# Cross-attention of a Perceiver layer on one core: row-tiled scores, own keys as a third chunk, row sums by ones

## The reference

```python
# x (64, 32, 128), context (64, 257, 256): 64 sequences, 32 queries, 257 context keys, 16 heads of 8
qkv = (x @ w_qkv.T).reshape(B, N, 3, H, D).transpose(2, 0, 3, 1, 4)
q, k, v = (qkv[0], qkv[1], qkv[2])
kv = context.reshape(B, N_c, 2, H, D).transpose(2, 0, 3, 1, 4)
k = jnp.concatenate([kv[0], k], axis=2)          # 257 context keys and the sequence's own 32
v = jnp.concatenate([kv[1], v], axis=2)
attn = jax.nn.softmax(jnp.einsum('bhnd,bhmd->bhnm', q * scale, k), axis=-1)
out = jnp.einsum('bhnm,bhmd->bhnd', attn, v)
out = out.transpose(0, 2, 1, 3).reshape(B, N, C) @ w_proj.T + b_proj
```

## Time and profile before

| what | value |
|---|---|
| median of 3 runs | 752.95 us (750.12 to 755.46) |
| the profiled execution | 755.94 us, of which the span is 754.2 us |
| mean granted TensorE clock in the span | 0.912 |
| TensorE busy | 622.8 us, 83% |
| VectorE, ScalarE, GpSimd busy | 465.4, 316.8, 399.6 us |
| sequence 0's first score, sequence 63's first score | 33.74, 341.36 us |

### The profile page before, as it was taken

The page is one execution under the profiler, slowest core; times in us unless marked ns, Lnnn a source line. Parts: engine busy times, 40 slices in busy tenths (PEclk is TensorE's granted clock), DMA queues, the critical chain, the costliest instruction groups (busy, mean ns, idle before and its releaser), DMA issues. The chain is left out here.

```text
span 754.2 us, 14892 instructions
## 1 busy us (share of the span) xinstructions
PE 622.8 (83%) x4426; PEld 428.6 (57%) x4426; DVE 465.4 (62%) x919; ACT 316.8 (42%) x1003; POOL 399.6 (53%) x685
## 2 busy tenths in 40 slices
PE   3899999999999999997487888889528464777993
PEld 2577777777777777775122222223216254766993
DVE  6077777777777777776628487696654912343446
ACT  3555555655555665552223151504015322343550
POOL 3155555555555555551535849373526666666540
PEclk9999999999999999999559998999956767998997
DMA  5014452121111112110000000000001011111216
GB/s 161 3 44 134 133 133 60 52 56 56 56 56 53 48 54 56 56 42 2 1 0 0 0 1 0 0 1 0 1 0 56 0 29 45 44 40 43 39 37 171
DMA packets 30472, 33.26 MB, mean 44 GB/s; under 512 B 3498, under 2 KB 20996, under 8 KB 30436
## 3 DMA queue, kind: packets, MB, share of 16 engines
q1 hardware_dynamic: 27940, 27.68, 13.0%
q0 software_dynamic: 2496, 5.12, 2.5%
HBM read 28.13 MB, written 4.65 MB: 43 GB/s over the span
## 5 line engine op out<-in xcount | busy, mean ns | idle before, releaser
L594 PE MATMUL psum<-kT,q_heads 128*128 128x289 f32 x512 | 145.9, 408 | 0.8 <-ACT kT L482 0.8
L639 DVE COPY pT<-psum 128x512 f32<-128x512 f32 x128 | 86.5, 676 | 73.3 <-PE psum L554 73.3
L499 ACT ACTIVATE probs<-psum,neg_max 128x289 f32<-128x289 f32 x256 | 126.1, 497 | 12.7 <-DVE inv_sum L672 2.3
L659 DVE TENSOR_REDUCE neg_max<-psum 128x2 f32<-128x578 f32 x128 | 96.7, 755 | 21.8 <-PE psum L594 19.8
L427 POOL TENSOR_TENSOR probs_own<-probs,ones 128x128 f32<-128x128 f32 x64 | 25.8, 404 | 134.9 <-ACT probs L499 134.9
L594 PEld LDWEIGHTS psum<-kT,q_heads 128*128 128x128 f32 x512 | 87.3, 190 | 16.1 <-issue 1.0
L554 PE MATMUL psum<-ident,probs 128*128 128x128 f32 x512 | 79.0, 277 | 0.9 <-ACT probs L499 0.8
L554 PEld LDWEIGHTS psum<-ident,probs 128*128 128x128 f32 x512 | 64.3, 152 | 11.3 <-ACT probs L499 1.6
L395 POOL TENSOR_TENSOR q_heads<-qT,head_scaled 128x512 f32<-128x512 f32 x64 | 67.2, 1050 | 6.1 <-ACT k_own L469 6.1
L479 ACT COPY pT_own<-psum 128x128 f32<-128x128 f32 x64 | 17.0, 266 | 119.6 <-PE psum L545 119.6
L836 POOL TENSOR_TENSOR read<-recep,state 128x496 f32<-128x496 f32 x32 | 44.7, 1397 | 39.6 <-DVE state L1058 39.6
(11 more groups left out here) (257 smaller groups left out, 1320.0 us busy)
## 6 DMA issues: line engine op xcount, KB each, us to landing
kv_in<-in_ctx SPq DMA_DIRECT2D x64, 256.0 KB
w_gate<-in_L_ffn_Wg SPq DMA_DIRECT2D x1, 1408.0 KB, 7.5
w_up<-in_L_ffn_Wu SPq DMA_DIRECT2D x1, 1408.0 KB, 6.7
x_res<-in_x SPq DMA_DIRECT2D x4, 256.0 KB, 3.7
v_left_in<-in_ctx SPq DMA_DIRECT2D x64, 2.0 KB
w_down<-in_L_ffn_Wd SPq DMA_DIRECT2D x2, 512.0 KB, 5.2
x_rows<-x_cen SPq DMA_DIRECT2D x4, 256.0 KB, 2.3
w_gate<-y_rows SPq DMA_DIRECT2D x4, 256.0 KB, 3.7
```

The costliest lines, as they stand in the source:

```text
L499: last = nc.scalar.activation(probs[:, par, gr, :], bank[S_BANK[h][k]][:, 0:KEYS], ACT.Exp, bias=neg_max[:, par, gr:gr + 1], accum_out=row ...
L594: last = pe.matmul(bank[S_BANK[h][k]][:, 0:KEYS], q_heads[:, par, HG * gr:HG * gr + HG, :].rearrange("p h n -> p (h n)"), kT[:, par, :], s ...
L639: nc.vector.tensor_copy(pT[:, par, h, :], bank[PT_BANK[h]][:]).then_inc(s_pT_out, 1)
L659: nc.vector.tensor_reduce(neg_max[:, par, 2 * h:2 * h + 2], psum[:, 2 * h:2 * h + 2, 0:KEYS], AX.X, ALU.max, negate=True).then_inc(s_max, 1)
```

## The change

- The scores: `q_heads` shrinks to 128 channels x (4 heads x 32 queries). A group of heads has its 32 channels on 32 partitions, and each of the four matmuls takes only those rows of `q_heads` and `kT` (32 rows, 128 columns), all four in one run and with one signal.
- The own 32 values of a sequence and the last context row's value lie on 33 partitions, from partition 0 for even and from 64 for odd sequences (`v_own`, copied in pairs to `v_now`). Their probabilities are turned by four transposes (`turn_own`) in the middle of `values`, and enter as a third chunk of 33 rows.
- The row sums are matmuls with `ones` as weights over the same three chunks, into columns 128 to 255 of `O_BANK`; the exponentials lose their accumulated output, and `inverse`, `spread` and the matmul of L574 go.
- The context's keys and values are two tiles and two DMAs (`k_in`, `v_in`). Keys are turned two sequences ahead, values are computed two behind; `first` and last steps that lack a part are written out (`PEELED`, `LAST`, `exists`).
- The copy of the first half of the probabilities goes from VectorE to ScalarE, as does the copy of `O_BANK` (`o_rows`); masking, sums over heads and the product with the inverse go to GpSimd, three and four sequences behind.
- The last context row's values are broadcast to 32 partitions per parity by two DMAs before the loop, and TensorE waits for them before it turns `k_left`. The own values' projection is 16 matmuls of 128 columns per block, in two halves and two banks; ScalarE and VectorE copy one half each.
- In the mixture of experts the ring of gathered token tiles, `NXS`, goes from 15 to 12. Some unused semaphores of the second block go.

The diff, cut to its core:

```diff
@@ tiles and the loop
-            kv_in = sb("kv_in", [P, NSLOT, KC, 2 * C], scope)
-            q_heads = sb("q_heads", [P, 2, H, N], scope)
+            k_in = sb("k_in", [P, NSLOT, KC, C], scope)
+            v_in = sb("v_in", [P, NSLOT, KC, C], scope)
+            q_heads = sb("q_heads", [P, 2, HG, N], scope)
...
+            def own_rows(par):
+                return slice(64 * par, 64 * par + N + 1)
@@ SyncE
+                left_rows = ctx_dram[:, NCTX - 1, C:2 * C].rearrange("(i r) c -> r i c", r=2)
+                for r in range(2):
+                    sp.dma_start(v_own_pairs[64 * r + N:64 * r + 2 * N, :, :],
+                                 left_rows[r:r + 1, :, :].broadcast_to([N, B // 2, C])).then_inc(s_left_in, 16)
...
+                def load_keys(b, u):
+                    if not first(b, NSLOT):
+                        sp.wait_ge(s_keys, b - NSLOT + 1)
+                    sp.dma_start(k_in[:, u, :, :], rows_of(b, slice(0, C))).then_inc(s_k_in[u], 16)
+                def load_values(b, u):
+                    if not first(b, NSLOT):
+                        sp.wait_ge(s_pv, b - NSLOT + 1)
+                    sp.dma_start(v_in[:, u, :, :], rows_of(b, slice(C, 2 * C))).then_inc(s_v_in[u], 16)
@@ GpSimd
+                def normalise(b, par):
+                    pool.wait_ge(s_o_rows, b + 1)
+                    g.tensor_tensor(o_masked[:], o_rows[:, par].rearrange("p s (h n) -> p s h n", h=HG),
+                                    head_in_group[:].unsqueeze(1).unsqueeze(3).broadcast_to([P, 2, HG, N]),
+                                    ALU.mult).then_inc(s_o_steps, 1)
...
+                def step(b, u):
+                    par = u % 2
+                    if exists(b + 1):
+                        ready_q(b + 1, 1 - par)
+                    if exists(b) and par == 0:
+                        ready_v(b, u)
+                    if exists(b - 4):
+                        attended(b - 4, par)
+                    if exists(b - 3):
+                        normalise(b - 3, 1 - par)
@@ ScalarE
                 def step(b, u):
                     par = u % 2
+                    if exists(b - 3):
+                        rows_out(b - 3, 1 - par)
+                    if exists(b - 1):
+                        probs_out(b - 1, 1 - par)
+                    if exists(b + 2):
+                        act.wait_ge(s_scores, b + 1)
+                        keys_out(b + 2, par)
+                    if exists(b):
+                        for h in range(2):
+                            act.wait_ge(s_max, 2 * b + (h + 1))
...
@@ TensorE
+                def keys(b, u):
+                    pe.wait_ge(s_k_in[u], loaded(b, u))
+                    if not first(b, 4):
+                        pe.wait_ge(s_own_out, b - 3)
...
+                def turn_own(b, par):
+                    start = KEYS - (N + 1) - 64 * par
+                    for gr in range(G):
+                        last = pe.transpose(KEY_BANK[0:KEYS - start, P * gr:P * gr + P], probs[:, par, gr, start:KEYS], ident[:])
+                    last.then_inc(s_own_T, 1)
+                def values(b, u, par, between=None):
+                    if not first(b, 1):
+                        pe.wait_ge(s_o_rows, b)
+                    if par == 0:
+                        pe.wait_ge(s_ready_v, b + 2)
+                    pe.wait_ge(s_v_in[u], loaded(b, u))
+                    pe.wait_ge(s_pT0_out, b + 1)
+                    pe.wait_ge(s_pT1_out, b + 1)
+                    pe.wait_ge(s_own_out, b + 1)
+                    mine = own_rows(par)
+                    for s in range(2):
+                        for c in range(KC):
+                            if s == 0 and c == 1 and between:
+                                between()
+                            for gr in range(G):
+                                rows = slice(N * gr, N * gr + N)
+                                pe.matmul(O_BANK[rows, P * s:P * s + P],
+                                          ones[:] if s else v_in[:, u, c, rows],
+                                          pT[:, par, gr // 2, P * (2 * (gr % 2) + c):P * (2 * (gr % 2) + c) + P],
+                                          start=(c == 0), stop=False, skip_group_check=True)
+                        for gr in range(G):
+                            rows = slice(N * gr, N * gr + N)
+                            last = pe.matmul(O_BANK[rows, P * s:P * s + P],
+                                             ones[mine, :] if s else v_now[mine, u // 2, rows],
+                                             pT_own[mine, P * gr:P * gr + P],
+                                             start=False, stop=True, skip_group_check=True)
+                    last.then_inc(s_pv, 1)
...
                 def step(b, u):
...
+                        pe.wait_ge(s_exp, 2 * b)
+                        for gr in range(G):
+                            rows = slice(N * gr, N * gr + N)
+                            last = pe.matmul(bank[S_BANK[gr]][:, 0:KEYS],
+                                             q_heads[rows, par].rearrange("p h n -> p (h n)"),
+                                             kT[rows, par, :], start=True, stop=True)
+                        last.then_inc(s_scores, 1)
+                    if exists(b + 2):
+                        keys(b + 2, (u + 2) % NSLOT)
+                    if exists(b - 1):
...
+                        turn_probs(b - 1, 1 - par, 1).then_inc(s_pT1, 1)
+                    if exists(b - 1) and exists(b - 2):
+                        pe.wait_ge(s_keys_out, b + 3 if exists(b + 2) else B)
+                        values(b - 2, (u + 2) % NSLOT, par, lambda: turn_own(b - 1, 1 - par))
...
+                        turn_probs(b, par, 0).then_inc(s_pT0, 1)
@@ VectorE: the two maxima of b, then for b - 1 the copy of the second half and of the own rows, then for b - 3 the inverse
+                        nc.vector.tensor_copy(pT[:, 1 - par, 1, :], bank[PT_BANK[1]]).then_inc(s_pT1_out, 1)
+                        nc.vector.tensor_copy(pT_own[mine, :], KEY_BANK[mine, :]).then_inc(s_own_out, 1)
+                        nc.vector.reciprocal(o_inv[:, 1 - par, :], o_sum[:, 1 - par, 1, :]).then_inc(s_o_inv, 1)
@@ mixture of experts
-            NXS = 15
+            NXS = 12
```

More of the change, by code:

```diff
@@ L439, in step @@
-                    if not first(b, 1):
-                        spread(b - 1, (u + 1) % 2)
-                for u in range(NSLOT):
-                    step(u, u)
+                    par = u % 2
[7 more added lines that the diff above has]
+                        normalise(b - 3, 1 - par)
@@ L452, in _ @@
-                pack_own(B - 1, 1)
-                spread(B - 1, 1)
+                for b in range(B - NSLOT, B + LAST):
+                    step(b, b % NSLOT)
             @block.scalar
@@ new lines, in rows_out, with probs_out @@
+                def rows_out(b, par):
+                    act.wait_ge(s_pv, b + 1)
+                    if not first(b, 2):
+                        act.wait_ge(s_o_steps, 2 * b - 3)
+                    nc.scalar.copy(o_rows[:, par], O_BANK[:, 0:2 * P].rearrange("p (s q) -> p s q", s=2)).then_inc(s_o_rows, 1)
+                def probs_out(b, par):
+                    act.wait_ge(s_pT0, b + 1)
+                    if not first(b, 2):
+                        act.wait_ge(s_pv, b - 1)
+                    nc.scalar.copy(pT[:, par, 0, :], bank[PT_BANK[0]]).then_inc(s_pT0_out, 1)
@@ L526, in _ @@
                     pe.matmul(bank[3][:], w_T[:, 1, :], ln_T[:, cols], start=True, stop=True).then_inc(s_proj, 1)
-                    if n:
-                        pe.wait_ge(s_v_own, n)
-                    for k in range(SPB):
-                        for gr in range(G):
-                            rows = slice(N * gr, N * gr + N)
-                            last = pe.matmul(bank[4][rows, N * k:N * k + C // G], ln_T[:, BLK * n + N * k:BLK * n + N * k + N],
-                                             w_T[:, 2, rows], start=True, stop=True, skip_group_check=True)
@@ L555, in turn_probs @@
                                                 probs[:, par, 2 * h + k, P * c:P * c + P], ident[:])
[L556 to L567 removed]
+                    return last
@@ L668, in inverse @@
-                def inverse(b, par):
-                    v.wait_ge(s_exp, 2 * b + 2)
-                    if not first(b, 2):
-                        v.wait_ge(s_spread, b - 1)
-                    nc.vector.reciprocal(inv_sum[:, par], row_sum[:, par]).then_inc(s_inv, 1)
+                for n in range(NB):
+                    v.wait_ge(s_proj, 4 * n + 4)
+                    pairs = slice(SPB // 2 * n + TPB, SPB // 2 * n + 2 * TPB)
+                    nc.vector.tensor_copy(v_own_pairs[0:N, pairs, :], bank[5][0:N, :].rearrange("p (i c) -> p i c", c=C))
+                    nc.vector.tensor_copy(v_own_pairs[64:64 + N, pairs, :],
```

(1 more changed line is left out.)

374 lines of the change are left out of this document (157 added, 217 removed).

## The result

The changed kernel takes 768.66 us (median of 4 runs, 766.98 to 772.6), the kernel before 751.54 us (4 runs, 748.84 to 755.46). The ratio is 1.023, with a 95% interval of 1.017 to 1.029. The forecast was 764. The profiled execution took 772.6 us with a span of 770.9, against 755.94 and 754.2.

What follows compares the result with a forecast made beforehand. TensorE's instruction passing was taken as the bound. At 5.02 us per sequence the loop takes 313.2 for 307.6; with tail 3.0 and head 2.8 that is +11.4, giving 764 on the 752.95 median; range 738 to 784.

Steps and rivals of the forecast that it cites:

- The list of instructions: TensorE, per sequence of the loop: all matmuls and transposes with shape changes and open weight loads, together 4.82 us.
- The gain on the scores: Score matmuls in the loop: four 32-row tiles side by side take 0.71 us for 1.95, saving 1.24 per sequence.
- The wait for the keys: TensorE before its value matmuls, per sequence: 0.08 us open, plus 0.12 for six satisfied waits behind it.
- The loop: Sequence 0's to sequence 63's first score: two steps of 3.5 and 61 of 5.02, 313.2 us for 307.6.
- The head: Before sequence 0's first score: 1.3 us for the last-row values' broadcast, 1.5 for the own values' projection, +2.8.
- a head more than 4 us later: Sign of a wrong forecast: the stretch before sequence 0's first score grows by over 4 us.
- The tail: From sequence 63's first score to the output projection: 12.3 us in place of 9.3, plus 3.0.
- Other engines and loads: In the loop ScalarE, VectorE and GpSimd hide under 5.02 us; DMA loads and the smaller gather ring cost nothing.
- A: Scores: the row tiles' weight loads pass one after another, 5.35 us per sequence, total 784; chance 0.13.
- B: Value matmuls: changes among 128-row and 64-row column tiles drain nothing, 4.74 us per sequence, total 747; chance 0.32.
- C: Loop: shape changes drain as priced, keys' wait and what follows cost nothing, 4.85 us per sequence, total 754; chance 0.15.
- D: Loop: the granted clock falls as TensorE has less column work; no chance of its own, would add to A.

Runs made afterwards that it cites:

- e2: Changed kernel with TensorE's wait for the copied keys moved to just before the fourth value matmul; step 4.740 us, ratio to before 0.9954.
- e3: Changed kernel with the own chunk's values and ones in one run after all 128-row chunks; step 4.836 us, ratio to before 1.0013.
- e4: Changed kernel with the scores alone back to four matmuls over 128 rows with masked queries; step 6.200 us, ratio to before 1.1226.
- e1: Changed kernel with TensorE's wait for the copied keys moved from first to last of the waits before the values; step 4.759 us, ratio to before 1.0008.
- e9: Changed kernel with two more satisfied waits behind the wait for the keys, hardware loop only; step 5.257 us, ratio to before 1.0318.
- e10: Changed kernel with 24 more sequences written out ahead of the hardware loop, waits against constants; step 4.983 us, ratio to before 1.0156.
- e6: Changed kernel with the left key's load apart from the left values' broadcast, which only GpSimd awaits; step 5.100 us, ratio to before 1.0181.
- e7: Changed kernel with row sums by ones over the own chunk alone, output scaled wrongly; step 4.403 us, ratio to before 0.9629.
- e8: Changed kernel with own chunk masked to 128 rows, value matmuls in one run, own transposes and keys' wait behind, plus e6's edit; 671.24 us, ratio 0.9279.

## Why the prediction was right

The direction, the places (head, loop, tail) and nearly the size were right: 764 forecast, 768.66 measured, slower by 2.3%, within the range. That the step came so near (5.02 for 5.10) is in part luck: the instructions were priced 0.16 too high and the wait with its queue 0.24 too low.

- **The list of instructions.** Forecast 4.82 us; e2, with its open 0.08 taken off, has 4.66. The scores came to 0.70 (0.71), a value chunk to 0.35 to 0.36 (0.36), the ones to 0.57 (0.58), the own transposes to 0.61 in even and 0.55 in odd sequences (0.59). The two runs of transposes behind a change were priced 0.05 to 0.06 too high each. That each change costs time is shown by e3.
- **The gain on the scores.** 1.24 forecast, 1.25 read, and e4 gives 1.10 for the step.
- **The wait for the keys.** The step that was mis-sized: "0.08 is open" plus "I take 0.12 as most of them can ride in pairs", 0.20 in all. It measured 5.10 − 4.66 = 0.44, above the bounds that the text gave (0.08 to 0.38). The wait itself was right: 0.10, by e1's 4.76. What stands behind it was wrong: 0.34 in place of 0.12. The text bounded each wait by 0.05; in the traces each item that is left, a wait or a register operation, takes about 0.1 us. Few are paired: of the changed kernel's items only one holds two satisfied waits. e1 moves them ahead and saves 0.34, e9 adds two and pays 0.15, e10 takes them away and gains 0.28. With the wait last, the loop is 9.5 us shorter than before (e1), in place of 7.7 longer.
- **The loop.** 7.7 for 5.6. Of that the 52 steps of the hardware loop are 4.4 us over the forecast (5.10 for 5.02), and the eleven steps at its ends 2.3 us under it, as the written-out ones take 4.8 and not 5.02. The forecast didn't tell the two kinds apart.
- **The head.** Forecast 1.3 for the broadcast and 1.5 for the own values; measured 4.15 (e6), and 1.26 for what is left. The two DMAs of 512 KB took 8.4 us to land, by the page's DMA issues, for 6.5 in the text, and nothing covered the end of it, as TensorE is in order and the left key's transpose stands ahead of the layer norm's. The upper bound in the text was 4, and I took a third of it for "partly beside other work", which no row showed. The head came 5.4 us later, and "a head more than 4 us later" stood among the text's own signs of being wrong.
- **The tail.** 3.0 forecast, 3.4 measured; the projection waits 2.83 us for GpSimd's last step, as listed.
- **Other engines and loads.** At nothing, and they cost nothing: behind the loop the two spans differ by 0.2 us, so the smaller ring of gathers doesn't show.
- **The rivals.** A (row tiles in line) falls: eight in 0.70. B (changes among column tiles free) falls: 0.13 each in e3. Its 0.32 was too much, as every change that the trace of before had cost 0.09. C (the wait and what follows it cost nothing) falls by the same 0.44; e1, level with before, shows that its total would have been right for another order of the statements. D: no fall of the clock in the loop. In the first steps it fell in six of eleven profiles of this family (e2, e3, e6, e7, e9 and e10), for up to 1.7 us.

In the account of the forecast's error of 5.3 us (11.4 for 16.7), the head has 2.6, the loop 2.1, the tail 0.4 and the later stages 0.2. Each is more than was forecast.

## What to carry to other kernels

On TensorE's queue put the wait that will block last, on the instruction that needs it: what stands behind it, satisfied or not, is paid after the release, in each step. Look in the trace for the order of the built program, since it isn't always that of the statements (e1's written-out steps, e9's fourth step). With small tiles count the changes of tile shape before the columns: the same 48 value instructions took 1.45 us in one run and 1.99 in five. Padding a 33-row chunk to 128 rows with masks costs TensorE no columns and spares the changes; GpSimd has two products in place of a copy, which in e8 didn't show.

## What the runs showed of the hardware

- A satisfied wait against a register's value, and the register operation beside it, take TensorE's queue about 0.1 us each where they stand behind a blocking wait (199.10 to 199.50 in the changed kernel); two more waits took 0.2 in the three steps of four in which they stand there (e9).
- Changes between 128-row, 64-row and 32-row tiles all cost: 0.09 from the distance of starts (0.20 for a pitch of 0.11), 0.13 with the open weight load of 32 columns (e3). "TensorEngine Tiling (Array Packing)" of the Trainium skill names the drain without a price.
- "PSUM — Partial Sum Buffer" of the Trainium skill says in section PSUM: the matmul accumulator that the `start` of a matmul clears the accumulation flags of the whole bank in the 32-partition quadrants that the matmul writes. By it, in e3 the `start` on columns 128 to 255 ended the accumulation of columns 0 to 127 of the same rows. The run agrees as far as it goes: its output is off by 0.21 of relative error, and no run isolates the cause.
- At the wait for the first exponentials (1.44 us; 1.56 in e4) the granted clock fell from 2.4 to 1.2 GHz in six profiles, within the wait or 0.3 us behind it, and stayed down for 3.4 us (e2, e3, e9) or 6.8 us (e6, e7, e10); it stayed up in five with the same wait. What decides it stays open.
